# Attention of a four-part layer stack: queries, keys, values and turned probabilities stored as rounded parts and rests, scores and values in three passes, gate weights loaded late

## What is computed

```python
q = (h @ Wq.T).reshape(b, s, 16, 128)   # h = layernorm(x)
k = (h @ Wk.T).reshape(b, s, 4, 128)    # four query heads share a key head
v = (h @ Wv.T).reshape(b, s, 4, 128)
scores = einsum("bhqd,bhkd->bhqk", q, k_rep)
attn = softmax(where(causal, scores, neg))
out = einsum("bhqk,bhkd->bhqd", attn, v_rep)
x = x + out.reshape(b, s, 2048) @ Wo.T + bo
```

## Time and profile before

| what | value |
|---|---|
| runs without profiler | 1223.6, 1227.35, 1232.17 us |
| profiled execution | 1228.41 us |
| its span | 1226.7 us, so 1.7 us lie around the span |
| PE busy in the span | 1124.7 us, 92% |
| DVE busy | 852.9 us, 70% |
| ACT busy | 637.3 us, 52% |
| POOL busy | 211.1 us, 17% |

### The profile page before, as it was taken

One profiled execution on the slowest core, in us unless ns is written; L12 is line 12 of the kernel. 1 busy time (PEld: TensorE's weight loads), 2 busy tenths in 40 slices (PEclk: granted clock), 3 DMA queues, 4 the chain that ended last, 5 costly groups with the idle time before them and its releaser, 6 DMA issues. The chain is left out here.

```text
span 1226.7 us, 26372 instructions
## 1 busy us (share of the span) xinstructions
PE 1124.7 (92%) x9980; PEld 963.5 (79%) x9980; DVE 852.9 (70%) x2427; ACT 637.3 (52%) x1596; POOL 211.1 (17%) x245
## 2 busy tenths in 40 slices
PE   3999999999999998999999999578799889898888
PEld 2799899889989987888888898456577667776767
DVE  4677567647856776667766757798889779777343
ACT  4654444444444443553444434456788688665341
POOL 0422132222222222430000000200220121021100
PEclk9999999999999998999999999678798798867789
DMA  9020000000000003001000000100000000000034
GB/s 311 2 70 2 1 1 1 1 1 1 2 1 1 1 1 95 1 1 28 1 1 1 1 1 30 57 30 3 32 30 3 31 31 30 3 2 3 25 94 141
DMA packets 26701, 32.90 MB, mean 27 GB/s; under 512 B 4960, under 2 KB 21968, under 8 KB 26576
## 3 DMA queue, kind: packets, MB, share of 16 engines
q1 hardware_dynamic: 24400, 29.12, 7.5%
q10 hardware_dynamic: 2176, 2.10, 0.5%
HBM read 29.04 MB, written 2.17 MB: 25 GB/s over the span
## 5 line engine op out<-in xcount | busy, mean ns | idle before, releaser
L365 DVE TENSOR_TENSOR a_ps<-a_ps,causal 128x256 f32<-128x256 f32 x128 | 54.7, 427 | 100.9 <-PE a_ps L635 100.9
L1537 PE MATMUL b_ps<-ln_high,b_high 128*128 128x512 f32 x256 | 101.6, 397 | 1.0 <-ACT gate_up_raw L1452 1.0
L683 PE MATMUL a_ps<-a_wo_high,a_oT 128*128 128x256 f32 x512 | 101.2, 282 | 0.1
L1537 PE MATMUL b_ps<-ln_low,b_high 128*128 128x512 f32 x256 | 100.8, 394 | 0.0
L1537 PE MATMUL b_ps<-ln_high,b_low 128*128 128x512 f32 x256 | 100.5, 392 | 0.0
L348 POOL TENSOR_TENSOR a_probs<-a_probs,a_inv 128x256 f32<-128x256 f32 x64 | 40.2, 627 | 339.9 <-DVE a_inv L385 339.9
L1571 PE MATMUL b_ps<-b_wd_high,b_mid 128*128 128x256 f32 x512 | 97.8, 286 | 0.0
L508 ACT ACTIVATE a_probs<-a_ps,a_negmax 128x128 f32<-128x128 f32 x128 | 47.1, 368 | 88.8 <-DVE a_negmax L371 79.5
L520 ACT CAST a_oT<-a_ps 128x512 fp32r<-128x512 f32 x64 | 37.5, 587 | 107.1 <-PE a_ps L661 107.1
L1452 ACT ACTIVATE gate_up_raw<-b_ps 128x512 f32<-128x512 f32 x64 | 37.4, 597 | 101.4 <-PE b_ps L1537 101.3
L1337 DVE TENSOR_TENSOR gate_up_raw<-gate_up_raw,b_ps 128x512 f32<-128x512 f32 x64 | 42.8, 685 | 62.8 <-ACT gate_up_raw L1452 34.2
(11 more groups left out here) (438 smaller groups left out, 3101.9 us busy)
## 6 DMA issues: line engine op xcount, KB each, us to landing
gate_up_raw<-a_scratch SPq DMA_DIRECT2D x8, 768.0 KB, 3.6
d_main<-in_D_main SPq DMA_DIRECT2D x14, 304.5 KB
x<-in_hidden SPq DMA_DIRECT2D x4, 512.0 KB, 10.6
a_raw<-in_A_q SPq DMA_DIRECT2D x4, 512.0 KB, 8.3
gate_up_raw<-in_A_o SPq DMA_DIRECT2D x1, 2048.0 KB
gate_up_raw<-in_B_g SPq DMA_DIRECT2D x1, 2048.0 KB, 12.2
gate_up_raw<-in_B_u SPq DMA_DIRECT2D x1, 2048.0 KB, 8.3
out<-x ACTq DMA_DIRECT2D x8, 256.0 KB, 2.2
```

What stands on the lines that cost most here:

```text
L365: nc.vector.tensor_tensor(diagonals, diagonals, r.causal[:].rearrange("p (o k) -> p o k", o=1).to_broadcast([P, 2, P]), ALU.add).then_inc( ...
L683: mm = nc.tensor.matmul(ps[:, out_bank(job), 0:HID], opart, wpart, start=(k == 0 and j == 0), stop=(k == QUARTER - 1 and j == len(passes) ...
L1537: mm = nc.tensor.matmul(ps[:, bank, :], wpart, xpart, start=(j == 0), stop=(j == len(passes) - 1))
```

## The change

1. **Parts and rests.** Queries, keys, values and turned probabilities become pairs of F32R tiles. ACT writes the rounded part out of PSUM and then signals `..._high_done`; DVE subtracts it from what is in PSUM and writes the rest (`lower_q`, `lower_k`, `lower_v`, `lower_pT`), and only then come q_taken, k_taken, v_taken and pT_copied, on which PE waits. The copy of the turned probabilities, which was DVE's, becomes two casts on ACT (`take_pT`) and two subtractions on DVE.
2. **Three passes.** Each product of scores and of values becomes three F32R products with the same shapes: 12 instructions in place of 4, for scores and for values of a head.
3. **Buffers.** `q` and `pT` have one buffer of each part instead of two of the whole. The rests of keys and values lie over `first_xnT` and over the gate weights' place.
4. **Late gate weights.** Two experts' gate weights (0.5 MB) are loaded as before. Four experts' (1 MB) are loaded when the values of the last head are done, two experts' (0.5 MB) right behind them; the experts stage waits for all three.

```diff
-        kT = later[:, 0:NKV * GROUP].rearrange("p (g t) -> p g t", t=GROUP)
-        qT = later[:, NKV * GROUP:(NKV + 2) * GROUP].rearrange("p (s t) -> p s t", t=GROUP)
...
+        k_high = by_head(over("k_high", kept.xnT_at, NKV * GROUP))
+        q_high, q_low = [over(x, kept.xnT_at + (NKV + k) * TILE, GROUP) for k, x in enumerate(("q_high", "q_low"))]
+        k_lows = [by_head(over(x, at, 2 * GROUP)) for x, at in (("k_low0", r.first_xnT_at), ("k_low1", gates_at))]
...
-        pT = sb("pT", [P, 2, GROUP_BATCHES, QW])
+        pT_high, pT_low = [sb(x, [P, GROUP_BATCHES, QW], F32R) for x in ("pT_high", "pT_low")]
...
-                next_weights.load(sp, 0)
+                next_weights.load(sp, 0, NLORA, NLORA + 2)
...
                 next_weights.load(sp, 1)
                 next_weights.load_router(sp)
+                sp.wait_ge(next_weights.loaded[0], 16)
+                sp.wait_ge(oT_ready, GROUPS * NH)
+                next_weights.load(sp, 0, NLORA + 2, NE)
+                sp.wait_ge(scores_ready, 2 * GROUPS * NH)
+                next_weights.load(sp, 0, 0, NLORA)
...
-                def copy_pT(G):
+                def lower_pT(G):
                     for b in range(GROUP_BATCHES):
-                        dve.wait_ge(pT_ready, 2 * G + b + 1)
-                        if G >= 2:
-                            dve.wait_ge(oT_ready, G - 1)
-                        nc.vector.tensor_copy(pT[:, G % 2, b, :], ps[:, PTB[b], 0:QW]).then_inc(pT_copied, 1)
+                        dve.wait_ge(pT_high_done, 2 * G + b + 1)
+                        nc.vector.tensor_tensor(pT_low[:, b, :], ps[:, PTB[b], 0:QW], pT_high[:, b, :].bitcast(F32),
+                                                ALU.subtract).then_inc(pT_copied, 1)
...
+                def lower_k(i, g):
+                    dve.wait_ge(k_high_done, i * NKV + g + 1)
+                    nc.vector.tensor_tensor(k_low[g], ps[:, PROJ[0], :], k_high[:, g, :].bitcast(F32), ALU.subtract
+                                            ).then_inc(k_taken, 1)
+
+                def lower_q(G):
+                    dve.wait_ge(q_high_done, G + 1)
+                    nc.vector.tensor_tensor(q_low, ps[:, PROJ[1], :], q_high.bitcast(F32), ALU.subtract
+                                            ).then_inc(q_taken, 1)
...
                     if h >= 1:
-                        copy_pT(G - 1)
+                        lower_pT(G - 1)
                     invert(G)
+                    if h + 1 < NH:
+                        lower_q(G + 1)
                     if G >= 2:
                         split_oT(G - 2)
                     for job in out_jobs(i, h)[0:1]:
                         add_out(job)
+                    if h == 0:
+                        for t in range(GROUP_TILES):
+                            lower_v(i, t)
+                    if 1 <= h < NKV:
+                        lower_k(i, h)
                     if i == 0 and 1 <= h <= SPLITS:
                         weight_lows(h - 1)
...
+                def take_pT(G, b):
+                    act.wait_ge(pT_ready, 2 * G + b + 1)
+                    if G >= 1:
+                        act.wait_ge(oT_ready, G)
+                    nc.scalar.copy(pT_high[:, b, :], ps[:, PTB[b], 0:QW]).then_inc(pT_high_done, 1)
...
                     exps(G, 0)
+                    if h >= 1:
+                        take_pT(G - 1, 0)
+                        take_pT(G - 1, 1)
                     exps(G, 1)
...
-                        nc.tensor.matmul(ps[:, SC[b], 0:P], q[:, chunk(b, 0)], k[:, chunk(b, 0)],
-                                         start=True, stop=True)
...
+                        for half, cols, keys_of in ((0, slice(0, P), chunk(b, 0)),
+                                                    (1, slice(P, QW), slice(2 * b * P, (2 * b + 2) * P))):
+                            rows = chunk(b, half)
+                            passes = split_passes(q[0][:, rows], q[1][:, rows], k[0][:, keys_of], k[1][:, keys_of])
+                            for j, (qpart, kpart) in enumerate(passes):
+                                mm = nc.tensor.matmul(ps[:, SC[b], cols], qpart, kpart,
+                                                      start=(j == 0), stop=(j == len(passes) - 1))
...
+                        for j, (vpart, ppart) in enumerate(firsts):
+                            nc.tensor.matmul(out, vpart, ppart, start=(j == 0), stop=False)
+                        for j, (vpart, ppart) in enumerate(seconds):
+                            mm = nc.tensor.matmul(out[:, P:2 * P], vpart, ppart, start=False, stop=(j == len(seconds) - 1))
```

More of the change, by code:

```diff
@@ L24 @@
 LN_EPS = 1e-5
+WORD = 4
 NEG = -1e30
@@ L205, in attention, with over, by_head, by_token @@
         later = kept.xnT[:].rearrange("p c t -> p (c t)")
-        kT = later[:, 0:NKV * GROUP].rearrange("p (g t) -> p g t", t=GROUP)
-        qT = later[:, NKV * GROUP:(NKV + 2) * GROUP].rearrange("p (s t) -> p s t", t=GROUP)
-        v_rest = later[:, (NKV + 2) * GROUP:(NKV + 4) * GROUP].rearrange("p (t n) -> p t n", n=NKV * HD)
-        v_first = ahead.xn[:].rearrange("p t d -> p (t d)").rearrange("p (t n) -> p t n", n=NKV * HD)
-        v = [half[:, t, :] for half in (v_first, v_rest) for t in range(GROUP_TILES // 2)]
+        def over(name, at, words):
+            return nc.alloc_sbuf_tensor_at("a_" + name, [P, words], F32R, offset=at)[:]
+        def by_head(x):
+            return x.rearrange("p (g t) -> p g t", t=GROUP)
+        def by_token(x):
+            return x.rearrange("p (t n) -> p t n", n=NKV * HD)
+        TILE = NKV * HD * WORD
+        gates_at, PAST_FIRST = next_weights.raw_at, (NLORA + 2) * DC * FE * WORD
+        k_high = by_head(over("k_high", kept.xnT_at, NKV * GROUP))
+        q_high, q_low = [over(x, kept.xnT_at + (NKV + k) * TILE, GROUP) for k, x in enumerate(("q_high", "q_low"))]
+        k_lows = [by_head(over(x, at, 2 * GROUP)) for x, at in (("k_low0", r.first_xnT_at), ("k_low1", gates_at))]
+        k_low = [half[:, g, :] for half in k_lows for g in range(NKV // 2)]
+        v_highs = [by_token(over(x, at, 2 * NKV * HD)) for x, at in (("v_high0", ahead.xn_at),
+                                                                    ("v_high1", kept.xnT_at + (NKV + 2) * TILE))]
+        v_high = [half[:, t, :] for half in v_highs for t in range(GROUP_TILES // 2)]
+        v_lows = by_token(over("v_low", gates_at + PAST_FIRST, GROUP_TILES * NKV * HD))
+        v_low = [v_lows[:, t, :] for t in range(GROUP_TILES)]
         negmax = sb("negmax", [P, 2, GROUP_TILES])
@@ L231, in attention @@
         bias_added, out_ready, out_taken = sem("bias_added"), sem("out_ready"), sem("out_taken")
+        k_high_done, q_high_done, v_high_done, pT_high_done = [sem(x) for x in "k_high_done q_high_done v_high_done pT_high_done".split()]
         M = {x: sem("m_" + x) for x in ahead.NAMES.split()}
@@ L288, in attention @@
         oT = sb("oT", [P, 2, RING, GROUP], F32R)
-        xn = kT[:, 0:2, :].rearrange("p g t -> p (g t)").rearrange("p (t d) -> p t d", d=HID)
+        xn = later[:, 0:GROUP_TILES * HID].rearrange("p (t d) -> p t d", d=HID)
         SPLITS = 4
@@ L446, in ln_low @@
                                             ).then_inc(M["ln_taken"], 1)
+                lower_k(0, 0)
+                lower_q(0)
                 for i, h in STEPS:
@@ L472, in _ @@
                         ln_normalise(i, h - 10)
+                    if h == NH - 1 and i < LAST_GROUP:
+                        lower_k(i + 1, 0)
+                        lower_q(G + 1)
                     if h == NH - 1:
-                        copy_pT(G)
+                        lower_pT(G)
                         add_out(out_jobs(i, h)[1])
@@ L487, in take_k @@
                         act.wait_ge(M["ln_turned"], DC * i)
-                    nc.scalar.copy(kT[:, g, :], ps[:, PROJ[0], :]).then_inc(k_taken, 1)
+                    nc.scalar.copy(k_high[:, g, :], ps[:, PROJ[0], :]).then_inc(k_high_done, 1)
                 def take_v(i, t):
@@ L566, in _ @@
                         take_q(G + 1)
+                    if h == NH - 1:
+                        take_pT(G, 0)
+                        take_pT(G, 1)
                 copy_oT(head(LAST_GROUP, NH - 1))
@@ L1061, in squares @@
                                      ).then_inc(self.S["square_ready"], 1)
+GATE_PARTS = 3
 class GateUpWeights:
@@ L1074, in __init__, with load @@
         self.router_loaded = ctx.enter_context(nc.semaphore("router_loaded"))
-    def load(self, sp, k):
-        sp.dma_start(self.raw[:, k], self.sources[k].rearrange("e (c p) f -> p e c f", p=P)
+    def load(self, sp, k, first=0, end=NE):
+        sp.dma_start(self.raw[:, k, first:end], self.sources[k][first:end].rearrange("e (c p) f -> p e c f", p=P)
                      ).then_inc(self.loaded[k], 16)
```

32 lines of the change are left out of this document (20 added, 12 removed).

## The result

| | before | changed |
|---|---|---|
| median | 1225.47 us (4 runs) | 1261.21 us (4 runs, 1255.33 to 1269.15) |
| ratio | | 1.032, 95% interval 1.0274 to 1.0366 |
| profiled execution: time, span | 1228.41, 1226.7 us | 1269.15, 1267.5 us |

The account below looks back on a forecast made before the run. PE, busy for 92% of the span, was taken as the bound. Groups 1 to 3 (27.5 us), group 0 (14.4) and the end (1.6) gave 43.5 us, added to 1228.4 for 1272 us; range 1236 to 1310.

Parts of the forecast that it names:

- likeliest case: DVE and ACT hand-offs hold PE up, plus a small price for its products: chance 0.63, own range 1250 to 1300.
- PE's products, +7.7: Scores and values on PE: three passes cost 0.12 us more per head, 7.7 us over 64 heads.
- "cheap" rival: On PE, 128-column F32R products cost 0.06 us, making the kernel faster, 1197 us; chance of faster 0.06.
- The relay in an ordinary head: PE's scores, DVE's maxima, ACT's exponentials and casts, DVE's queries' rest: in time with 0.26 us to spare, no gap.
- T: The time at which DVE starts a head's mask, 0.86 us after PE starts that head's scores.
- Heads 1 to 3 of groups 1 to 3, +1.38 each: Keys' products wait for DVE's late out-job addition: 1.38 us more in each of nine heads, 12.4 us.
- S: The time at which PE starts a head's scores.
- Heads 10 to 13, +1.75 per group beyond the products: DVE's root links in head 10 and L439 in heads 11 to 13 delay the queries: 1.75 us per group.
- Head 14, +1.35: The turning of the next input on PE waits for DVE's out-job addition: 1.35 us.
- Group 0, +14.4: First group: 9.9 us in heads 1 to 5, from keys' rests, weight_lows and late probabilities, and 4.5 in the rest.
- fall of the clock: In group 0, PE's idle times might bring 1.2 GHz: 10 us more, 1300 us, as an upper bound.
- The end, +1.6: Behind the last head, values wait 0.6 us for both parts of pT, and late loads cost 1 us.

Follow-up runs that it names:

- e2: The changed kernel with DVE's addition of the out job moved ahead of the rest of the queries: 1255.51 us, ratio 1.0259.
- e11: The changed kernel with POOL's addition of group 0's output bias moved from head 2 to head 0: 1259.79 us, ratio 1.0277.
- e5: The kernel before with only the late gate-weight loads of the change: 1220.67 us, ratio 0.9988.
- e10: e9 with POOL's addition of group 0's output bias moved from head 2 to head 0: 1217.1 us, ratio 0.9935.
- e9: e8 with the queries' rest ahead of the out job's addition in most heads, group 0's keys' rest behind the probabilities' rests: 1217.51 us, ratio 0.9951.
- e3: The changed kernel with the rest of the keys taken in the next head, between the two batches' maxima: 1250.96 us, ratio 1.0225.
- e8: The changed kernel with the out job's addition earlier, the keys' rest later, and 128-column products in full F32: 1221.95 us, ratio 1.0007.

## Why the prediction was right, and where its terms were off

The forecast (1272, slower with 0.81) holds: the measured median lies in the range and in the likeliest case's own, 11 us below the forecast: 36 us more than before, where I had 43.5. The profiled execution gave 1269.15, 40.8 above that of before by the spans. The mechanism is the one that I had worked out; that the sum came so close is in part luck, as the terms show. By its steps, each against the head table:

- **PE's products, +7.7.** The mechanism is right: 0.11 apart, and the third pass at 128 eats what 256 saves. Measured is 0.16 per ordinary head, not 0.12, about 10 us: a batch takes 0.69 where I had 0.68, the scores' first, which doesn't stand behind a product of 256, 0.75, and the values' first 0.64 (202.42 to 203.06). The "cheap" rival came true for three of a head's twelve products of 128 columns only, those behind a product of 256, and each of them is offset by a product of 256 that takes 0.17 behind one of 128; with that its 1197 fell. The Trainium skill (TensorE: Matmul & The Clock Gate, "LDWEIGHTS (loading the stationary operand)") gives P/1.2 ns, 107 for 128 columns, for such a load, which the spacing of 0.11 agrees with; the N/2.4 + 2.5 gap, which "Back-to-back issue gap" gives for an isolated product, fits only the product behind one of 256 columns, 0.06.
- **The relay in an ordinary head.** I had the rest of the queries done at T + 4.95; with T = 217.16 in a head of group 1 it ended at 222.04, T + 4.88. Ordinary heads have no gap, as said.
- **Heads 1 to 3 of groups 1 to 3, +1.38 each.** Measured +1.36, +1.49, +1.48, with gaps of 1.02, 1.14 and 1.15 on PE, released by DVE's addition to x. e2 shows the cause. Inside, two small errors cancel in head 1: the addition ended 0.11 earlier than I had it (S + 7.22), and from the start of the keys' products to the next scores it is 1.47 us, not 1.39.
- **Heads 10 to 13, +1.75 per group beyond the products: the term that failed.** Measured is 0.3 beyond them. I carried over the durations of the earlier trace rows: 0.72 for L439 and 0.58 for the first link of the root. In the changed kernel, DVE and POOL in head 10 of group 2:

```profile
347.23 0.16 DVE L465 TENSOR_TENSOR ln_t<-ln_r 128x4 f32<-128x4 f32 x1
...
348.02 0.41 DVE L477 TENSOR_SCALAR all_xnT<-x,ln_mv,ln_t 128x256 f32<-128x256 f32 x1
```

```profile
346.04 1.04 POOL L374 TENSOR_TENSOR a_probs<-a_probs,a_inv 128x512 f32<-128x512 f32 x1
```

  Before, POOL's second product ran to 315.75, over the link at 315.18 that took 0.58:

```profile
314.71 1.04 POOL L350 TENSOR_TENSOR a_probs<-a_probs,a_inv 128x512 f32<-128x512 f32 x1
```

  Now it ends at 347.08, ahead of the link: DVE's later work had moved out from beside it, and 0.42 and 0.31 us came back. The durations that I added up were those of a collision that the change itself takes apart. They are not all of it. Head 11 took 6.49 where I had 7.36, and 0.42 of these 0.87 is the link; the 0.2 that I had added to T of head 11 stands in no row. In heads 11 and 12 DVE's round is 6.04 and 6.10 where I had 6.48, and 0.31 of that is L439; it stays below PE's 6.23, so nothing is lost there. Of the gap that I had named before the scores, released by DVE's rest of the queries, 0.10 us is left, once a group.
- **Head 14, +1.35.** Measured +0.72, products included. I had it follow from T being late in that head, and that from the same two durations.
- **Group 0, +14.4.** Measured 16.2. Heads 2 to 5 of my working were 8.66, 8.66, 7.71 and 6.65; measured 8.56, 10.55, 8.20 and 7.20. The fall of the clock, which I had only as a bound, came twice, in head 3 behind a wait of 2.54 us that ended at 59.63, and in heads 4 and 5 behind one of 2.18 that ended at 69.83 (windows of the changed kernel):

```profile
59.63:62.60 2.97, 2.97 (x13) 2.90 (x14) 1.78 (x4) 1.21 (x5) 1.61 (x2) 0.52 0.00 0
69.83:76.80 6.97, 6.97 (x32) 6.87 (x33) 5.48 (x12) 3.16 (x10) 1.61 (x2) 0.51 0.35 99
```

  The granted clocks of 0.52 and 0.51 are the level of 1.2 GHz for nearly all of these windows. Head 3 without it takes 8.64 (e11), 1.9 less. Of that 0.3 is a shorter wait, since the values there begin 5.82 after the scores in place of 6.13, so the clock is worth about 1.6 in head 3; heads 4 and 5 are together 1.0 above my working. Head 0 cost 1.05 where I had counted its products alone; PE waits 0.90 us in it for the rest of the queries.
- **The end, +1.6.** Measured 0.7: 0.2 from the last head's scores to the last out job, and half a microsecond behind it. The loads are free, as e5 shows alone. At the other end, the first scores wait 1.40 us for the rest of the queries where they waited 0.68 for the copy, which I had not counted; they begin 0.6 later.

So two errors of opposite sign nearly cancelled: heads 10 to 14 too dear by some 8 us over four groups, PE's price and group 0's first six heads too cheap by 6. The sum was closer than its terms, and that is luck.

## What to carry to other kernels

When a copy becomes cast plus rest on two engines, look at what stands behind the new wait on the second engine, before its own cost: here 31 of 40 us came with the rests, and 24 of them went when two pieces of DVE's work changed places with their neighbours. Three passes pay for products of 256 columns (0.35 against 0.44) and not for those of 128 (0.33 against 0.22), so splitting by shape (e10) beat both kernels, the one before by 0.65%. And a duration read beside another engine's work holds only while that work stays beside it: look at what overlaps a row before adding it up.

## What the runs showed of the hardware that I had not expected

- A subtraction of DVE with both inputs in SBUF and POOL's addition run one after the other, and whichever begins second waits: DVE 3.38 in place of 1.22 us, ending 1.09 after POOL's instruction (e9), or POOL 3.38 in place of 2.40 with DVE undisturbed at 1.27 (e3). The Trainium skill (SBUF — State Buffer, "Who interferes with whom") says that a DVE instruction with two SBUF inputs contends with a GpSimd instruction that reads SBUF, and that the order of issue decides who blocks; the rows of e9 and e3 agree.
- PE waited 0.18 us in each ordinary head of e8 with no idle time shown, because the modelled end of the last matmul covered it; e9 gave it back, and 0.1 in the scores behind it.
- A wait of 2.09 us was followed by a clock of 1.00 in one program and 0.75 in another, in which one POOL instruction had moved two heads earlier (the change and e11).
- Switching PE between full F32 and F32R products costs next to nothing in the sum: in e10 scores take 1.16 and values 1.15, 2.31 against 2.28 for their products alone. By the starts, the first F32R product of 256 columns behind an F32 one does take 0.20 in place of 0.12, but the F32 product of 128 ahead of it 0.14 in place of 0.22 (values, 177.21, 177.35 and 177.55). I had allowed 0.08 for each switch.
